# Graph convolution, attention and experts on one core: expert weights spread by transfers and multiplied in on GpSimd, a third room for the early pairs, and a new order of steps

## What is computed

```python
# layer 0: graph convolution with temporal and spatial attention
E = softmax(V_e @ sigmoid(prod)); x_tat = x @ E
S = softmax(V_s @ sigmoid(prod2))
out = sum_k  einsum(cheb[k] * S, x) @ Theta[k]
y = relu(residual(x) + temporal_conv(relu(out)));  y = layernorm(y)
# layer 1a: causal linear attention, 16 heads of 16
phi = elu(.) + 1;  out_t = (phi_q S_t) / (phi_q z_t + eps);  S_t = running sum of phi_k v^T
# layer 1b: experts. 16 experts of width 64, 4 chosen per token in 2 of 4 groups, and a shared part of width 512
w = the 4 chosen sigmoid scores, divided by their sum, 0 elsewhere      # (token, expert)
h = silu(x gate) * (x up)                                               # per expert
out = shared + sum over experts of (h * w) down
```

## Time and profile before

| | |
|---|---|
| Three runs | 986.01, 986.10 and 988.42 us, median 986.1 us |
| The profiled execution, its own time | 988.29 us |
| Its span, first to last instruction | 986.5 us |
| PE busy | 928.2 us, 94% of the span |
| DVE, ACT, POOL busy | 602.0 us (61%), 413.6 us (42%), 207.0 us (21%) |
| Mean granted clock of TensorE | 0.98 of full |
| Chain that ended last | PE 83%, DVE 7%, ACT 6%, issue 2%, POOL 1%, DMA 1% |

### The profile page before, as it was taken

How to read it: one execution, slowest core, us unless ns; L and a number is a source line. 1 busy time by engine, 2 the same in 40 slices (tenths; PEclk the granted TensorE clock), 3 DMA queues, 4 the chain that set the end, 5 groups by cost and what they waited for, 6 DMA issues and landing times.

```text
span 986.5 us, 20130 instructions
## 1 busy us (share of the span) xinstructions
PE 928.2 (94%) x8254; PEld 823.7 (83%) x8254; DVE 602.0 (61%) x1630; ACT 413.6 (42%) x796; POOL 207.0 (21%) x184
## 2 busy tenths in 40 slices
PE   5697879999999999999999999999999999999997
PEld 3486657988978989798988989788898889888997
DVE  4648865756685377744786467852778447764532
ACT  3543513722564226551365415642265523622431
POOL 2004100022401123121312123011231213112222
PEclk9799889999999999999999999999999999999999
DMA  9100000000000100001000010000000000000000
GB/s 324 49 1 22 1 1 1 2 23 13 1 12 1 33 2 11 2 1 33 2 12 2 1 33 1 12 2 30 5 12 1 2 12 1 12 1 12 12 12 11
DMA packets 14378, 17.78 MB, mean 18 GB/s; under 512 B 1073, under 2 KB 12721, under 8 KB 14289
## 3 DMA queue, kind: packets, MB, share of 16 engines
q1 hardware_dynamic: 14288, 16.51, 5.0%
HBM read 12.31 MB, written 4.19 MB: 17 GB/s over the span
## 4 chain that ended last, share of the span: by engine, by line
PE 83%; DVE 7%; ACT 6%; issue 2%; POOL 1%; DMA 1%; SPq 0%; POOLq 0%; DVEq 0%; ACTq 0%
PE ring L1314 8%; PE d_ps L506 5%; PE g_ps L506 5%; PE d_ps L507 4%; PE d_ps L508 4%; PE g_ps L508 4%; PE u_ps L507 4%; PE u_ps L508 4%; PE u_ps L506 4%; PE g_ps L507 4%; PE ring L1182 4%; PE ring L1297 3%; PE num L1211 3%; PE ring L506 3%; PE ring L508 3%; PE ring L507 3%
## 5 line engine op out<-in xcount | busy, mean ns | idle before, releaser
L652 POOL TENSOR_TENSOR hl<-hb,hh 128x512 fp32r<-128x512 f32 x96 | 122.9, 1281 | 492.2 <-ACT hh L796 492.2
L1150 DVE TENSOR_TENSOR hb<-sl,u_ps 128x512 f32<-128x512 f32 x88 | 60.2, 684 | 109.8 <-PE u_ps L508 47.9
L506 PE MATMUL d_ps<-hh,down_h 128*128 128x256 f32 x384 | 113.5, 296 | 1.9 <-POOL hl L652 1.9
L506 PE MATMUL g_ps<-normed_h,gate_h 128*128 128x256 f32 x352 | 109.3, 310 | 0.4 <-DVE hb L1154 0.2
L507 PE MATMUL d_ps<-hl,down_h 128*128 128x256 f32 x384 | 107.5, 280 | 0.0
L508 PE MATMUL d_ps<-hh,down_l 128*128 128x256 f32 x384 | 107.5, 280 | 0.0
L796 ACT ACTIVATE hh<-hb 128x512 fp32r<-128x512 f32 x96 | 60.9, 634 | 108.1 <-DVE hb L1154 88.6
L508 PE MATMUL g_ps<-normed_h,gate_l 128*128 128x256 f32 x352 | 99.2, 282 | 0.0
L507 PE MATMUL u_ps<-normed_l,up_h 128*128 128x256 f32 x352 | 99.1, 282 | 0.0
L508 PE MATMUL u_ps<-normed_h,up_l 128*128 128x256 f32 x352 | 99.1, 282 | 0.0
L506 PE MATMUL u_ps<-normed_h,up_h 128*128 128x256 f32 x352 | 99.1, 281 | 0.0
(11 more groups left out here) (340 smaller groups left out, 2144.5 us busy)
## 6 DMA issues: line engine op xcount, KB each, us to landing
out_x<-kept SPq DMA_DIRECT2D x16, 256.0 KB, 2.1
x_s<-in_x SPq DMA_DIRECT2D x14, 256.0 KB, 3.0
raw_weights<-in_gateT SPq DMA_DIRECT2D x4, 384.0 KB, 8.4
raw_weights<-in_upT SPq DMA_DIRECT2D x4, 384.0 KB, 9.8
raw_weights<-in_down SPq DMA_DIRECT2D x4, 384.0 KB, 12.4
cheb_s<-in_cheb SPq DMA_DIRECT2D x3, 256.0 KB, 4.7
raw_weights<-in_wqkvT SPq DMA_DIRECT2D x2, 384.0 KB, 6.4
shared<-in_x SPq DMA_DIRECT2D x2, 256.0 KB, 2.8
```

Of the source, the lines that this page charges most:

```text
L506: eng.matmul(ps, wh, xh, start=start, stop=False, **how)
L652: pool.tensor_tensor(hl[:, j % 2, :], hb, hh[:, j % 2, :].bitcast(F32), ALU.subtract).then_inc(*ffn_pool.mark(p, f"lo{j}"))
L1150: dve.tensor_tensor(hb, sl, gate_up(p, j)[1][:, :], ALU.mult).then_inc(*ffn_dve.mark(p, f"h{j}"))
```

## The change

Four things change together.

1. **How the expert weights reach the hidden units.** The matrix `spread` and the L1475 matmuls are gone. `cb` transposes one part (16 x 512, full float32), ACT copies it to `comb`; SP writes comb to a DRAM buffer, waits until it has landed, and then, for each routed step, issues two transfers that read the two rows of each chunk and write them over 64 partitions each, into one half of the buffer `over` (128 x 2 x 512, two routed steps deep).
2. **Who multiplies.** hb = hb * over is now a POOL instruction, right ahead of POOL's own subtraction; ACT's rounding waits for POOL in routed steps, and the DVE instruction L1154 is gone. PE's next `gu` now waits for `h{j}` alone. SP walks the same list of steps as the other engines, where it had a loop of its own.
3. **A third room.** Pair 1 has a room of its own in raw_weights (small buffers in sl and hb), so the first three pairs have three rooms. Only four of the now 14 pieces of weights are loaded at the start; the other ten wait for the end of pair 1's tail (`z3`), since they lie in that room. The roundings of the pieces are steps `high0` to `high13` and `low0` to `low13` of the list.
4. **A new order** in OPENING, BODY and CLOSING, with 24 in place of 23 `hot` steps.

```diff
+CHAINS["high"] = [f"high{i}" for i in range(14)]
+CHAINS["low"] = [f"low{i}" for i in range(14)]
+ROOMS = 3
...
-    +1 tok0 tok1 lg nrm +1 gn +2 xg xl0 +1 xl1 +1 r1 +2 xT0 M k0 k1 v1 xT1 +1 Y0 r2 q0 r3 v0 kt q1 prod silu +1 r4 +1
+    +1 tok0 tok1 lg +1 gn +1 nrm xg +4 r1 +1 xT0 xl0 xl1 M r2 xT1 +2 k0 k1 v1 q0 v0 r3 +2 Y0 silu +1 r4 prod cb Epre
...
-        spread = sb("spread", [P, ROUTED, P], F32R)
+        ones = sb("ones", [P, P], F32R)
+        over = sb("weights_over_hidden", [P, 2, 512])
...
         rooms = [conv_room(shared[:, 0:3072], shared[:, 3072:6144], shared[:, 6144:7168], shared[:, 7168:7680], shared[:, 2816:3008]),
+                 conv_room(raw[:, 3072:6144], raw[:, 6144:9216], raw[:, 9216:10240], sl, hb),
...
+        comb = sb("comb", [EXPERTS, 512])
+        rows_kept = nc.dram_tensor("weights_by_expert", (2, EXPERTS, 512), F32).ap()
...
             for i in range(len(PIECES)):
+                if i == EARLY_PIECES:
+                    sp.wait_ge(tail_dve.of(1), tail_dve.at(1, "n30"))
+                    sp.wait_ge(tail_pool.of(1), tail_pool.at(1, "n31"))
                 sp.dma_start(PIECES[i][3], PIECES[i][0]).then_inc(piece_loaded[i], 16)
...
+            def keep_rows(p):
+                sp.wait_ge(route_act.of(p), route_act.at(p, "cb"))
+                sp.dma_start(rows_kept[p % 2], comb[:, :]).then_inc(rows_written, 16)
+                sp.wait_ge(rows_written, 16 * (p + 1))
+
+            def spread_rows(p, r):
+                j = ROUTED_STEPS[r]
+                if p or r > 1:
+                    user = (p, ROUTED_STEPS[r - 2]) if r > 1 else (p - 1, ROUTED_STEPS[r - 2])
+                    sp.wait_ge(ffn_pool.of(user[0]), ffn_pool.at(user[0], f"w{user[1]}"))
+                first = 2 * chunks_of(j)[0]
+                toks = slice(j // HALF * L, (j // HALF + 1) * L)
+                for e in range(2):
+                    source = rows_kept[p % 2].rearrange("(c e) l -> e c l", e=2)[e, first // 2:first // 2 + 2, toks]
+                    sp.dma_start(over[64 * e:64 * e + 64, r % 2].rearrange("p (c l) -> p c l", c=2),
+                                 source.unsqueeze(0).to_broadcast([64, 2, L])).then_inc(over_loaded[r % 2], 16)
...
             def ffn(p, kind, j):
+                if kind == "w" and routed(j):
+                    r = ROUTED_STEPS.index(j)
+                    pool.wait_ge(over_loaded[r % 2], 32 * (p * len(ROUTED_STEPS) // 2 + r // 2 + 1))
+                    pool.wait_ge(ffn_dve.of(p), ffn_dve.at(p, f"h{j}"))
+                    pool.tensor_tensor(hb, hb, over[:, r % 2, :], ALU.mult).then_inc(*ffn_pool.mark(p, f"w{j}"))
                 if kind == "w":
 
                     pool.wait_ge(ffn_act.of(p), ffn_act.at(p, f"hi{j}"))
...
-                    act.wait_ge(ffn_dve.of(p), ffn_dve.at(p, f"w{j}" if routed(j) else f"h{j}"))
+                    if routed(j):
+                        act.wait_ge(ffn_pool.of(p), ffn_pool.at(p, f"w{j}"))
+                    else:
+                        act.wait_ge(ffn_dve.of(p), ffn_dve.at(p, f"h{j}"))
...
-                if kind == "w" and routed(j):
-                    dve.wait_ge(ffn_pe.of(p), ffn_pe.at(p, f"cm{j}"))
-                    dve.wait_ge(ffn_dve.of(p), ffn_dve.at(p, f"h{j}"))
-                    dve.tensor_tensor(hb, hb, gate_up(p, j)[0][:, :], ALU.mult).then_inc(*ffn_dve.mark(p, f"w{j}"))
...
-                if kind == "h" and routed(j):
-
-                    pe.wait_ge(route_act.of(p), route_act.at(p, "cb"))
-                    pe.wait_ge(ffn_act.of(p), ffn_act.at(p, f"si{j}"))
-                    for x, chunk in enumerate(pair):
-                        last = pe.matmul(gate_up(p, j)[0][:, x * L:(x + 1) * L], spread[:, chunk, :], comb[:, toks], start=True, stop=True)
-                    last.then_inc(*ffn_pe.mark(p, f"cm{j}"))
```

More of the change, by code:

```diff
@@ new lines @@
+    2:Erep 0:v0 0:kt 0:q1 0:hot16 1:tc1 0:hot17 2:lr 1:z1 0:dent 2:p2 0:hot18 0:kv 1:z2 0:rd 0:S00 2:sp0 0:V00 1:z3
+    2:rv0 0:S01 0:hot19 2:sp1 0:at0 0:V01 0:high4 0:S10 0:low4 0:hot20 0:V10 0:low5 0:S11 2:st0 0:hot21 0:high5
+    0:high6 2:rv1 0:V11 0:at1 2:Y1 0:low6 0:wo0 0:wo1 0:hot22 0:high7 0:tk0 0:tk1 0:nrm2 2:st1 2:o0 0:xn0 0:xn1 0:low7
+    1:tok0 0:hot23 0:high8 0:lg 0:r1 +1 1:tok1 +1 0:high9 0:high10 1:nrm 2:o1 0:low8 1:xl0 0:low9 1:xl1 0:r2 +1 0:r3
+    0:high11 0:low10 2:tc0 +1 0:high12 +1 0:low11 0:silu 1:k0 0:r4 1:k1 1:v1 2:tc1 +2 1:q0 0:cb 1:v0 1:kt 1:q1
@@ L196, in routed @@
     return chunks_of(j)[0] < ROUTED
+ROUTED_STEPS = [j for j in range(STEPS) if routed(j)]
 GROUPS = [f"{b}{lc}" for b in range(2) for lc in range(2)]
-NO_TILE = ["xg", "Eexp", "rv0", "rv1", "nrm", "nrm2", "at0", "at1", "exp", "silu"] + ["V" + g for g in GROUPS] + CHAINS["tail"] + CHAINS["ffn"] + CHAINS["warm"] + "lg r1 r2 r3 r4 cb".split()
+NO_TILE = ["xg", "Eexp", "rv0", "rv1", "nrm", "nrm2", "at0", "at1", "exp", "silu"] + ["V" + g for g in GROUPS] + CHAINS["tail"] + CHAINS["ffn"] + [n for c in ONCE for n in CHAINS[c]] + "lg r1 r2 r3 r4 cb".split()
 RING = 4
@@ L439, in graph_attention_moe @@
         ffn_pe = Signal(sem("ffn_by_pe"), in_order("ffn", {
[L440 removed]
+            **{f"gu{j}": f"g{j} u{j}" for j in steps}, **{f"dn{j}": f"dn{j}" for j in steps[:-1]}}))
         last_down = Signal(sem("last_down_by_pe"), ["dn"])
@@ L534, in graph_attention_moe @@
                            raw[:, wide * (10 + k):wide * (11 + k)].rearrange("p (c n) -> p c n", c=3)))
-        ONE_PART = 3 + 4
+        ONE_PART = 3 + 5
         BOTH_PARTS = 3 + 8
-        ROUTED_DOWN = {2: 13, 3: 14, 4: 15, 5: 15}
-        HIGH_AT = {"0:xT1": 2, "0:Epre": 2, "0:p2": 2, "1:Epre": 2, "0:rv1": 1, "0:Y1": 2, "1:Y1": 2, "1:o0": 2}
-        LOW_AT = {"0:Erep": 2, "0:p2": 2, "1:p2": 2, "0:st1": 2, "1:st1": 6}
-        def splits(p, name, at):
-            here = f"{p}:{name}"
-            if here not in at:
-                return []
-            order = [w for w in (f"{q}:{n}" for q, n in PROGRAM) if w in at]
-            before = sum(at[n] for n in order[:order.index(here)])
-            return range(before, before + at[here])
-        PREP_POOL = 12
-        assert len(PIECES) == sum(HIGH_AT.values()) == sum(LOW_AT.values()) + 1
+        ROUTED_DOWN = {2: 13, 3: 14, 4: 14, 5: 14}
+        PREP_POOL = 11
+        assert len(PIECES) == len(CHAINS["high"]) == len(CHAINS["low"])
         block = ctx.enter_context(nc.Block())
@@ L579, in prefetch @@
                 for b in range(2):
-                    sp.dma_start(rooms[1].x_s[:, b], x_v[p, b]).then_inc(x_loaded, 16)
-            def store(p):
-                for b, done in ((0, ffn_dve), (1, second_half)):
-                    sp.wait_ge(done.of(p), done.at(p, f"out{b}"))
-                    sp.dma_start(out_v[p, b], x1_at(p)[:, :, b, :]).then_inc(out_stored[p % 3], 16)
-            for p in range(2, PAIRS):
-                prefetch(p)
-                if p >= 3:
-                    store(p - 3)
@@ L590, in _, with store @@
-            for p in range(max(PAIRS - 3, 0), PAIRS):
-                store(p)
+                    sp.dma_start(rooms[ROOMS - 1].x_s[:, b], x_v[p, b]).then_inc(x_loaded, 16)
+            def store(p, b):
+                done = second_half if b else ffn_dve
+                sp.wait_ge(done.of(p), done.at(p, f"out{b}"))
+                sp.dma_start(out_v[p, b], x1_at(p)[:, :, b, :]).then_inc(out_stored[p % 3], 16)
+            def keep_rows(p):
+                sp.wait_ge(route_act.of(p), route_act.at(p, "cb"))
+                sp.dma_start(rows_kept[p % 2], comb[:, :]).then_inc(rows_written, 16)
+                sp.wait_ge(rows_written, 16 * (p + 1))
@@ new lines, in _ @@
+            for p, name in PROGRAM:
+                if name == "xb" and ROOMS - 1 <= p < PAIRS - 1:
+                    prefetch(p + 1)
+                if name in ("out0", "out1"):
+                    store(p, int(name[3]))
+                if name == "cb":
+                    keep_rows(p)
+                    spread_rows(p, 0)
+                    spread_rows(p, 1)
+                if name[0] == "w" and name[1:].isdigit() and int(name[1:]) in ROUTED_STEPS[:-2]:
+                    spread_rows(p, ROUTED_STEPS.index(int(name[1:])) + 2)
```

170 lines of the change are left out of this document (84 added, 86 removed).

## The result

| | before | after |
|---|---|---|
| Median (4 runs each) | 987.3 us | 974.7 us |
| Ratio, with its 95% interval | | 0.987 (0.985 to 0.990) |
| Profiled execution, its own time | 988.3 us | 975.9 us |
| Its span | 986.5 us | 974.3 us |
| From pair 0's `cb` copy to the end of the span | 789.6 us | 790.8 us |

The last line is the whole result in one number. Pair 0's copy stands at 196.87 us in the trace before and at 183.54 after: the opening gave 13.3 us, as forecast (-13). Behind that copy 128 matmuls and their waits are gone, and the time is 1.1 us longer. (The forecast was made from three runs of the kernel before, median 986.1 us; with the fourth the median is 987.3.)

A forecast was written before the change was run, and what follows sets the result against it. PE bounds the middle (98.2 of 100 us busy), pair 0's chain the opening. Terms -15.3 - 14 + 14 + 0.6 - 5 - 13 + 2 = -30.7 took 988.3 to 957.6, by median 955.4, stated 956 us; 8-in-10 range 942 to 977.

The forecast's parts named there:

- The opening, -13: Up to pair 0's first gate steps: new order, earlier z3 and filled gaps save 13 us, bounds 0 and 22.
- Its sign post: Pair 0's gu0 should start near 152 us, not 174.5; after 165 would show the forecast wrong.
- The longer chain through hb, +0.6: From h to hl, POOL's product takes 0.6 us more; covered in middle pairs, only the very end pays 0.6 us.
- The round trip, +14: From cb to dn2, through DRAM: 9.9 us against 7.9 of cover, 2 us wait in seven pairs, 14 us.
- The waits of the spreading matmuls, -14: In the middle, waits for silu 5.1, copy to comb 4.9 and issue 4.0 us go: 14 us saved.
- The spreading matmuls, -15.3: In PE's queue, 128 matmuls of 0.119 us go, on the path throughout: 15.3 us saved.
- The order of a turn, -5: Waits for the next pair's statistics and for copies freeing a bank behind Y0: 5 of 7.5 us saved.
- POOL beside DVE, +2: POOL's 64 added instructions slow DVE's beside them, about 1 us a pair on DVE; 2 us on the path.
- the one through hb: Rival, chance 0.07: h{j+1} waits in DVE's queue for POOL; 64 steps at 1.3 us cost 83 us, time 1039.

The follow-up runs named there:

- b1: The change's transfers and POOL's product, with the order and two rooms of the kernel before: 990.5 us, ratio 1.002 to the kernel before.
- a3: The change's order and three rooms, but spreading matmuls (at step h, for the first routed step at w) and DVE's product, no transfers: 1033.2 us.
- d1: The change with the product of h and weights on DVE instead of POOL: 958.97 us, ratio 0.971 to the kernel before.
- s1: The change without the write to DRAM and the spreading transfers; POOL's product multiplies by a constant 0.25: 969.5 us.
- s2: The change without the write to DRAM and the spreading transfers, the product by a constant 0.25 on DVE: 957.5 us.
- b2: The order and two rooms of the kernel before, with the change's transfers and the product on DVE: 1004.0 us.
- d4: The change with the product on DVE, and POOL doing one extra unneeded product behind its subtraction in each routed step: 964.6 us.
- h2: The change with POOL's product written over the block of weights, so that hb is free behind the product: 975.0 us.

## Why the prediction was wrong

- *The opening, -13: right in size.* -13.3 at pair 0's copy, and b1 and a3 show that it comes with order and rooms and not with the transfers. Of its pieces, POOL's half of `z3` ends 8.5 us sooner (82.2 for 90.8, "some 9" forecast), but DVE's half now ends at 84.0, so the whole step is 6.7 sooner. The other pieces were not tried apart. Its sign post was missed: pair 0's first gate matmul starts at 157.8 us, not near 152.
- *The longer chain through hb, +0.6: here it failed.* The step was "In a middle pair PE has between `gu{j}` and `dn{j}` at least 4.3 us of work (order), mostly over 7", and for pair 7 "So the cycle keeps the gain. Only the very end pays". The chain's length was right (4.2 forecast, 4.16 measured), but it is as long as the cover that the step names. A chain of 3.5 us fits under 4.3 with room for a late start or a slowed instruction (4.04 at 688.68), one of 4.2 does not (4.62 at 695.58). It cost 15.7 us with all that goes with POOL's product (d1), 12.0 of them also without the round trip (s1 and s2), against the 0.6 + 2 of the sum. "At least" was read as "enough" for steps that stand back to back, and 4.2 against 4.28 in pair 7 as "under". The cycles of pair 7's later routed steps, which the sum had at 4.28, are 4.25 to 4.78 us in the change and 4.25 in d1; those of its first two are 6.2 and 6.0, through the round trip.
- *The round trip, +14: too much.* 5.2 us with POOL's product, 1.5 with DVE's. Each piece was sized near the mark; the cover ahead of `dn2` was taken too low, and pair 7 was left out.
- *The waits of the spreading matmuls, -14: misread.* The sum 5.1 + 4.9 + 4.0 counts the same stretches twice. In pair 5 of the kernel before:

```profile
754.35 0.30 PEld L1475 LDWEIGHTS g_ps<-comb,spread 128*128 128x128 f32 x2 [0.98 <-ACT comb L786]
754.38 0.47 PE L1475 MATMUL g_ps<-comb,spread 128*128 128x256 f32 x2 [0.82 <-ACT sl L793]
```

  PEld's 0.98 us and PE's 0.82 are one wait, and the 4.0 us of issue are PEld's alone but for one. What PE lost is the 5.1 us of its own rows; all its idle time in this stretch is 15.0. The 9 us too many here and the 9 us too many for the round trip cancel by luck.
- *The spreading matmuls, -15.3: not a term of its own.* In the old order their removal is worth nothing with POOL's product (b1) and costs 17 us with DVE's (b2). In the new one their presence costs 58 us against the change, and 74 against d1, whose product is also DVE's; 28.5 of them are PE's waits at the gate bank in the middle. The rows of the waits told what PE waited for, not what would be late next.
- *The order of a turn, -5: not seen.* The 7.5 us of waits went, and `kept` 3.9 and `filters` 3.1 us came.
- *POOL beside DVE, +2: too small, as far as is known.* d4 has 5.6 us for it, with what else comes late in POOL's queue.

Of the rivals, the one through hb had the right mechanism and the wrong waiter. It priced 64 routed steps at 1.3 us and put the threshold at 0.47; measured are 15.7 / 64 = 0.25 us a step, and DVE's queue behind hb is not it (h2). The range (942 to 977) held the time because it reached to other cases, not because one of them happened. From pair 0's copy on the forecast had -17.7 us. The run with the product on DVE has 958.2 - 183.7 = 774.5 us there, 15.1 less than before: what was forecast for the change is close to what the change gives without POOL's product. That is in part luck, since the terms behind it (-14, +14, -5) did not come one by one.

## What to carry to other kernels

Compare a chain with its cover at the steps that have the least of it, and do not count a margin of 3% (4.2 under 4.3) as cover: here 0.64 us added to a chain of 3.5 cost 15.7 us in all, with what goes with it. Idle time of an engine does not say that work may be moved to it; POOL was 79% idle, and with the new order the wrong place for the product, because `dn` waits for the result. In the old order it was the better place, and as far as the rows show because the wait for the transfer then lies in POOL's queue and not in DVE's. And the part of an order that is written out for one mechanism has no price apart from it: try both changes together and each alone before either is given one. Last, do not add PE's waits and PEld's: they can be one stretch of time.
